# Pairing the value products of a five-layer attention kernel in every second position

## The reference

```python
# L0: 8 heads, layer norm on both inputs, residual
x = x + attn(ln(x) @ Wq.T, ln(c) @ Wk.T, ln(c) @ Wv.T)
# L1: 16 heads, causal, and masked by lengths, residual
x = x + attn(x @ Wq.T, c @ Wk.T, c @ Wv.T)
# L2: 16 heads, then Wo, residual, and a GELU network of width 512 (tanh form), residual
x = x + attn(...) @ Wo + bo;  x = x + gelu(x @ W1 + b1) @ W2 + b2
# L3, first half (L3S here): 16 heads, causal self-attention, Wo, residual, layer norm
x = ln(x + attn(x, x) @ Wo1 + bo1) * g1 + b1
# L3, second half (L3C here): 16 heads on the context, Wo, residual, layer norm,
# a GELU network (erf form), residual, layer norm
x = ln(x + attn(x, c) @ Wo2 + bo2) * g2 + b2
x = ln(x + gelu(x @ W1 + bf1) @ W2 + bf2) * g3 + b3
```

## Time and profile before

| | |
|---|---|
| runs | 534.62, 534.72, 537.14 us; median 534.72 us |
| the profiled execution | 539.41 us, span 537.7 us |
| TensorE busy (PE) | 478.6 us, 89% of the span |
| VectorE (DVE), ScalarE (ACT), GpSimd (POOL) | 397.6 (74%), 329.1 (61%), 215.9 us (40%) |
| mean granted TensorE clock | 0.948 of 2.4 GHz |

### The profile page before, as it was taken

How to read it: one execution, slowest core, us unless ns; L and a number is a source line. 1 busy time by engine, 2 the same in 40 slices (tenths; PEclk the granted TensorE clock), 3 DMA queues, 4 the chain that set the end, 5 groups by cost and what they waited for, 6 DMA issues and landing times.

```text
span 537.7 us, 17167 instructions
## 1 busy us (share of the span) xinstructions
PE 478.6 (89%) x6720; PEld 296.5 (55%) x6720; DVE 397.6 (74%) x1093; ACT 329.1 (61%) x662; POOL 215.9 (40%) x256
## 2 busy tenths in 40 slices
PE   1457779879999999999999999999999999999973
PEld 1346556545555555556666666655555556666652
DVE  6456788756778877878888866887788987788451
ACT  1434465435665666677777666666666677788841
POOL 2633376643543224344444444333443333522233
PEclk9956799787999999999999999999999999999997
DMA  4494434332343343322232222223333231220000
GB/s 116 87 265 86 119 74 109 83 75 65 83 88 79 76 94 78 83 64 62 63 67 67 64 61 62 63 67 81 83 68 83 68 87 47 61 62 14 12 21 20
DMA packets 71886, 40.45 MB, mean 75 GB/s; under 512 B 7004, under 2 KB 71548, under 8 KB 71680
## 3 DMA queue, kind: packets, MB, share of 16 engines
q1 hardware_dynamic: 71808, 39.36, 31.2%
HBM read 4.74 MB, written 1.05 MB: 11 GB/s over the span
## 4 chain that ended last, share of the span: by engine, by line
PE 73%; DVE 9%; DMA 4%; ACT 4%; issue 4%; SPq 3%; POOL 3%; POOLq 0%; DVEq 0%; ACTq 0%
PE o_ps L953 16%; PE attn_ps L926 14%; PE misc_ps L974 5%; PE misc_ps L983 5%; PE misc_ps L960 4%; PE misc_ps L888 4%; PE misc_ps L894 4%; PE score_ps L809 4%; PE misc_ps L889 3%; PE misc_ps L966 3%; PE misc_ps L970 2%; DMA pairs<-max_rows 2%; SPq L426 2%; PE misc_ps L905 2%; PE score_ps L842 2%
## 5 line engine op out<-in xcount | busy, mean ns | idle before, releaser
L738 DVE TENSOR_REDUCE max_words<-score_ps 128x4 f32<-128x512 f32 x288 | 195.8, 685 | 64.6 <-PE score_ps L842 62.9
L638 ACT ACTIVATE probs<-attn_ps 128x512 f32<-128x512 f32 x288 | 169.7, 596 | 96.7 <-PE attn_ps L926 92.2
L519 POOL TENSOR_TENSOR rest<-qk_f,terms 128x512 f32<-128x512 f32 x40 | 46.3, 1158 | 200.7 <-ACT terms L589 200.7
L953 PE MATMUL o_ps<-probs,v 128*32 128x128 f32 x2304 | 123.9, 288 | 0.0
L842 PE MATMUL score_ps<-pairs 52*128 52x128 bf16 (+1 forms) x1152 | 117.2, 224 | 6.3 <-DMA pairs<-terms 6.3
L926 PE MATMUL attn_ps<-pairs 55*128 55x128 bf16 (+1 forms) x1152 | 115.4, 222 | 5.8 <-DMA pairs<-max_rows 4.0
L926 PEld LDWEIGHTS attn_ps<-pairs 55*128 55x128 bf16 (+1 forms) x1152 | 65.5, 96 | 54.0 <-issue 30.4
L842 PEld LDWEIGHTS score_ps<-pairs 52*128 52x128 bf16 (+1 forms) x1152 | 69.0, 97 | 8.8 <-DMA pairs<-terms 7.0
L953 PEld LDWEIGHTS o_ps<-probs,v 128*32 128x32 f32 x2304 | 45.7, 108 | 43.3 <-issue 14.2
L527 POOL TENSOR_TENSOR terms<-rest,terms 128x512 bf16<-128x512 f32 x40 | 46.7, 1168 | 7.9 <-DVE max_words L751 5.9
L521 POOL TENSOR_TENSOR terms<-qk_f,terms 128x512 bf16<-128x512 f32 x40 | 46.3, 1157 | 0.0
(11 more groups left out here) (107 smaller groups left out, 745.6 us busy)
## 6 DMA issues: line engine op xcount, KB each, us to landing
pairs<-terms SPq DMA_DIRECT2D x240, 128.0 KB
w<-in_weights_dram SPq DMA_DIRECT2D x1, 1984.0 KB, 9.9
x_tok<-in_x_dram SPq DMA_DIRECT2D x8, 128.0 KB, 2.8
c_tok<-in_ctx_dram SPq DMA_DIRECT2D x8, 128.0 KB, 2.7
pairs<-max_rows SPq DMA_DIRECT2D x64, 12.0 KB
out_dram<-x_tok SPq DMA_DIRECT2D x8, 128.0 KB, 1.8
pairs<-constant_rows SPq DMA_DIRECT2D x4, 112.0 KB
row<-in_rows_dram SPq DMA_DIRECT2D x1, 320.0 KB, 4.6
```

What stands on the lines that cost most here:

```text
L519: pool.tensor_tensor(rest[:, :, :], qk_f32[:, :, :], terms[:, :, 0, :], ALU.subtract)
L638: act.activation(probs[n % PROBS_RING][:, :, :].rearrange("p h q -> p (h q)"), attn_ps[n % 2][:, :], ACT.Exp, scale=float(D // HEADS[part] ...
L738: dve.tensor_reduce(max_words[ub(step) % 2][:, QUAD * g:QUAD * (g + 1)], score_ps[n % 2][:, :].rearrange("p (h k) -> p h k", h=QUAD), AX_X ...
L953: last = pe.matmul(o_ps[32 * j:32 * j + 32, region * P:(region + 1) * P], values, probs[n % PROBS_RING][:, j, :], start=part == L0 or g % ...
```

## The change

In the 16-head parts a group with an even number has its `pv` one position later, so that groups 0 and 1, and 2 and 3, come one behind the other in positions 3, 5, 7 and 1. `o_tr` comes two positions after `o_evac`, and the entries of `CHAIN` are moved to odd positions where they use TensorE, and further from attention: `w2` of L2 from 26 to 31, the store of L3C from 30 to 37. With that all of TensorE's steps but `attn`, `score` and their masks stand in odd positions. `probs` gets a sixth buffer, and `attn_tok`, `stats` and `var_eps` a second.

```diff
-PROBS_RING = 5
+PROBS_RING = 6
...
-    L3S: (("qk", -25), ("split", -25), ("rest", -24), ("term1", -23), ("term2", -22), ("v", -14)),
+    L3S: (("qk", -25), ("split", -25), ("rest", -24), ("term1", -23), ("term2", -22), ("v", -13)),
...
-O_TR_AFTER = {L0: 1, L1: 1, L2: 1, L3S: 1, L3C: 1}
+O_TR_AFTER = {L0: 1, L1: 2, L2: 2, L3S: 2, L3C: 2}
...
-    L2: (("a_tr", 12), ("wo", 13), ("w1", 15), ("w1", 15), ("square", 17), ("square", 18), ("cube", 18),
-         ("cube", 19), ("tanh", 21), ("tanh", 21), ("gelu", 21), ("gelu", 22), ("w2_first", 25), ("w2", 26)),
-    L3S: (("a_tr", 11), ("wo", 13), ("x_tr", 16), ("x_stats", 18), ("x_norm", 19), ("x_back", 22)),
-    L3C: (("a_tr", 11), ("wo", 13), ("x_tr", 14), ("x_stats", 15), ("x_norm", 17), ("x_back", 19), ("w1", 21),
-          ("w1", 21), ("w2_first", 23), ("w2", 24), ("x_tr", 27), ("x_stats", 28), ("x_norm", 30), ("out", 30),
-          ("store", 30)),
+    L2: (("a_tr", 13), ("wo", 15), ("w1", 19), ("w1", 19), ("square", 21), ("square", 22), ("cube", 22),
+         ("cube", 23), ("tanh", 25), ("tanh", 25), ("gelu", 25), ("gelu", 26), ("w2_first", 31), ("w2", 31)),
+    L3S: (("a_tr", 13), ("wo", 15), ("x_tr", 17), ("x_stats", 19), ("x_norm", 20), ("x_back", 23)),
+    L3C: (("a_tr", 13), ("wo", 15), ("x_tr", 17), ("x_stats", 18), ("x_norm", 20), ("x_back", 23), ("w1", 25),
+          ("w1", 25), ("w2_first", 29), ("w2", 29), ("x_tr", 33), ("x_stats", 35), ("x_norm", 37), ("out", 37),
+          ("store", 37)),
...
-RANK = {"attn": -2, "w2": 17, "score": 2, "nmax": 11, "n_tr": 15, "o_tr": 16, "load": 20, "ln_in": 20,
+RANK = {"attn": -2, "w2": 31, "score": 2, "nmax": 11, "n_tr": 15, "o_tr": 16, "load": 20, "ln_in": 20,
...
-                put(pos + PV_AFTER[part], Step("pv", u, b, g))
+                put(pos + PV_AFTER[part] + (1 - g % 2 if part > L0 else 0), Step("pv", u, b, g))
...
-        attn_tok = sb("attn_tok", [P, PAIR, D])
+        attn_tok = [sb(f"attn_tok{r}", [P, PAIR, D]) for r in range(2)]
```

More of the change, by code:

```diff
@@ L225, in build @@
         cnT = [sb(f"cnT{r}", [P, TOK]) for r in range(2)]
-        stats = sb("stats", [P, 2 * PAIR, 6])
+        stats = [sb(f"stats{r}", [P, 2 * PAIR, 6]) for r in range(2)]
         mean_var_ring = [sb(f"mean_var{r}", [P, 2 * PAIR, 2]) for r in range(LN_RING)]
-        var_eps = sb("var_eps", [P, 2 * PAIR])
+        var_eps = [sb(f"var_eps{r}", [P, 2 * PAIR]) for r in range(2)]
         rstd_ring = [sb(f"rstd{r}", [P, 2 * PAIR]) for r in range(LN_RING)]
@@ L510, in _ @@
                     pool.wait_ge(var_ready, n + 1)
-                    pool.tensor_scalar(var_eps[:, 0:k], mean_var_ring[n % LN_RING][:, 0:k, 1], eps, None, ALU.add)\
+                    pool.tensor_scalar(var_eps[n % 2][:, 0:k], mean_var_ring[n % LN_RING][:, 0:k, 1], eps, None, ALU.add)\
                         .then_inc(eps_added, 1)
                     pool.wait_ge(eps_added, n + 1)
-                    pool.tensor_tensor(rstd_ring[n % LN_RING][:, 0:k], var_eps[:, 0:k], minus_half[:, 0:k], ALU.pow)\
+                    pool.tensor_tensor(rstd_ring[n % LN_RING][:, 0:k], var_eps[n % 2][:, 0:k], minus_half[:, 0:k], ALU.pow)\
                         .then_inc(rstd_ready, 1)
@@ L670, in _ @@
                     for k, src in enumerate(srcs):
-                        last = dve.bn_stats(stats[:, k, :], src)
+                        last = dve.bn_stats(stats[n % 2][:, k, :], src)
                     last.then_inc(stats_done, 1)
@@ L674, in _ @@
                     for k in range(len(srcs)):
-                        last = dve.bn_aggr(mean_var_ring[n % LN_RING][:, k, :], stats[:, k, :])
+                        last = dve.bn_aggr(mean_var_ring[n % LN_RING][:, k, :], stats[n % 2][:, k, :])
                     last.then_inc(var_ready, 1)
@@ L760, in _ @@
                     dve.wait_ge(recip_done, ub(step) + 1)
-                    dst = attn_tok[:, b, :].rearrange("p (h e) -> p h e", e=d)
+                    dst = attn_tok[u % 2][:, b, :].rearrange("p (h e) -> p h e", e=d)
                     spread = recip[:, 0:heads].unsqueeze(2).to_broadcast([P, heads, d])
@@ L965, in _ @@
                     for k in range(PAIR):
-                        last = pe.transpose(bank[:, k * P:(k + 1) * P], attn_tok[:, k, :], ident[:, :])
+                        last = pe.transpose(bank[:, k * P:(k + 1) * P], attn_tok[u % 2][:, k, :], ident[:, :])
                     last.then_inc(misc_ready, 1)
```

## The result

The changed kernel took **544.15 us** (median of 4 runs, 539.31 to 554.85) against 535.93 for the kernel before (4 runs, 534.62 to 539.04): a ratio of **1.0125, 95% interval 1.0071 to 1.0179**. Six more runs on another chip gave 542.49 us and 1.0134 (1.0095 to 1.0173). So it is slower by 1.3%, where I had forecast 526.5 us. Medians and ranges take in every run; a ratio and its interval leave out the runs over 1.5% above their kernel's fastest.

A forecast was written before the change was run, and what follows sets the result against it. The prediction took TensorE to bound L1 to L3C, and a chain of waits the end. By parts, -4.0 - 4.1 + 2.4 - 7.3 + 4.8 = -8.2 us took 534.7 to 526.5 us, range 513 to 535.

The forecast's parts named there:

- Term 1: TensorE, L1 to L3C: 250 fewer changes of array mode at 0.09 us each, 22.5 us less.
- Rival E: TensorE: a change of mode is not what costs, 17 us of the saving go, 543 us; chance 0.04.
- Term 2: GELU network's work runs later, moving between parts: L2 -1.9 us, L3S +1.9, L3C -3.2.
- term 7: The end: `x_back` of the last unit falls 4.8 us later after attention, 26.4 becomes 31.2 us.
- Term 3: New TensorE waits in L2, 1.2 us a full unit: +6.5 us in L2, +2.6 in L3S; 2 of old waits go.
- Term 4: L3S: `x_norm` waits for GpSimd and delays VectorE's second reduction, 0.4 us on six units, +2.4.
- Term 5: L3C: TensorE waits for the exponential behind the second table load, 13.3 us a unit in 35 to 39; net +3.7.
- Term 6: L1: the maxima's way through the DMA, 3.2 us, stays hidden behind TensorE's work, by 0.2 us.
- D: VectorE comes one reduction later than walked at two places a unit, L2 to L3C: 19 us, 546 us; chance 0.11.
- B: Waits charged in L2, L3S and L3C hardly come: 10 of 15 us fall away, 516.5 us; chance 0.28.
- C: GpSimd holds VectorE's `nmax` in seven full-chain units, 0.9 us each: 6.3 more, 533 us; chance 0.11.

The follow-up runs named there:

- e1_pairs: The kernel before with only the pairing of the `pv` steps and the sixth `probs` buffer: 530.94 us, ratio 0.9885.
- e10_v: The changed kernel with `v` of L3S two positions later, in position 5 instead of 3: 540.64 us, ratio 1.0076 to the kernel before.
- e11_xnorm: The changed kernel with `x_norm` of L3S one position later, behind VectorE's reduction: 537.88 us, ratio 1.001 to the kernel before.

## Why the prediction was wrong

**Term 1 (250 changes of mode at 0.09 us) was right**, and a little small. Two `pv` in a row start 0.24 us apart (0.27 taken), busy time from L1 on fell by 23.1 us, and e1_pairs shows that the pairs alone bring 6 us of the kernel's time, 10 together with the rest of the change. Rival E is refuted. The Trainium skill, page TensorEngine Tiling (Array Packing), Tiling Modes, says that a change of mode drains the engine; the rows agree, 0.23 us for a block ahead of another and 0.32 ahead of a transpose.

**Term 2 and term 7.** The matmuls moved as told (8 more start in L3S, 16 fewer in L3C and 16 more in the end); no run prices them by themselves. The end took 30.0 and 32.8 us for 31.2.

**Term 3, L2: the size, and a wait that I did not see.** I walked 13.2 us for a full unit, and units 20 and 21 take 13.26, with 0.89 us before `w2` for 0.6. But I walked one unit and used it for all. From unit 22 on `v` of L3S stands in position 3, with `o_tr` and both `w1`, and three banks later the second `w1` gets the bank of that position's `o_tr`: 1.0 us in each of units 22 to 25, 4.0 us (e10_v). The diff had moved that `v` from -14 to -13, and I had put no price on it. Nor did 2 us of old waits go on balance: in L2 before, `o_tr` waited 1.1 us and the attention blocks 1.6, for reductions and at issue; the first is gone, but the blocks now wait 3.4, for reductions, exponentials and at issue.

**Term 4, L3S: the size.** I put 0.4 us on six units. `x_norm` costs 0.7 in units 27 to 30, more in 26 and 31, and 0.8 in each of units 32 and 33, which are L3C's (e11_xnorm): 6.5 us for 2.4. I had the mechanism; its price was not worked out from rows, and the units of L3C were left out.

**Term 5, L3C: the walk was right, its neighbours were not.** Units 36 and 37 take 13.41 us for the 13.3 walked, with 1.0 us before the block of position 4; unit 38 takes as long with 1.9 us there. But units 32 to 34 take 10.6, 10.6 and 10.2, where 94.2 for the part leaves 9.2 each: L3S's `x_norm` again, and a reduction in position 4. With e10_v's unit 35 (13.94) and 39 (13.13), both at full clock, L3C makes 98.6 us, 4.4 over the forecast.

**Term 6 was wrong by its margin.** Hidden by 0.2, I said, from a sum of seven durations. The row of waits shows five waits of up to 0.8 us for the maxima's DMA in L1. In unit 9:

```profile
132.44 0.76 SPq L442 DMA_DIRECT2D pairs<-max_rows  x1
...
135.64 0.23 PE L809 MATMUL attn_ps<-causal_t,ident_bf 32*32 32x128 bf16 x4 [0.76 <-DMA pairs<-max_rows]
```

The block goes on 3.2 us behind the DMA's issue (2.3 to 3.4 in the five units), where I had taken 2.22 for the landing, from one row; what makes it longer stays open. L1 came out as forecast only because its units were shorter otherwise: 10 and 12, without such a wait, take 9.6 and 9.7 us for 10.0 to 10.1.

**A term was missing: the clock.** In the earlier trace rows PEclk is 1.00 from L2 to L3C. In the changed kernel it falls to half in four stretches there, and in both of its profiles unit 35 takes 15.5 us (13.94 at full clock) and unit 39 15.8 (13.13): 4.2 us in L3C alone. Over all executions the changed kernel has 15 us more at half clock than before; at the 0.26 us each that are fitted below, that is an estimated 4 us.

Summed for the profiled execution: 4.0 (bank of `w1`) + 4.1 (`x_norm` beyond term 4) + 4.2 (clock in L3C) are 12.3 of the 14.5 us missed from L1's start on. The other 2.2 are a net of misses both ways: 2.1 more in L2, where the waits of the blocks grew, and 2.9 in L3C, where units 32 to 35 were longer still, against 1.6 less in L3S and 1.3 in L1 and the end. By the medians the change cost 5.6 to 8.2 us where I had forecast a gain of 8.2, a miss of 14 to 16.

**The rivals.** D was the nearest: VectorE later than walked at the places where TensorE wants a bank from it, 546 us forecast with a chance of 0.11, 544 measured. That its number came so near is luck: at its two places `n_tr` of position 5 waits 0.7 us in all and `w2` up to 0.3 more than walked, far from its 19 us, and the loss lies at `w1`, the masks of L3S, the blocks of L3C and the clock. I held against it that VectorE is at 83% at most. As I read it, that was the error behind the terms: each wait is set by what stands ahead of one instruction, and a mean over a part does not bear on it. B, on the same mean, had 0.28. C (GpSimd holding `nmax`) did not come at its place: in the changed kernel the `nmax` of L2 take 0.17 to 0.18 us from unit 19 on. But the rows show the thing itself, with the waits of e1_pairs behind it, and in units 9 to 14 of the changed kernel, where L748 takes 0.86 us beside a GpSimd instruction and no wait of TensorE for it appears. Both signs that I had named against myself came, the waits for the maxima's DMA in L1 and units of L2 over 13.5 us (22 and 23: 14.2 and 15.3).

## What to carry to other kernels

When steps are gathered into one place, price the result twice: the gain by what the gathering saves (here 6 to 10 us), and the loss by walking every distinct kind of unit, the seams between parts above all, up to the first instruction that empties a bank for another engine. A step that waits for a third engine (`x_norm`) must stand behind what TensorE waits for, never ahead, however idle its engine is on average. And try tables part by part: the whole change lost 1.3%, and its tables chosen by part, with a handful of numbers moved, gained 2.8%.
